# ALiBi attention: the bias enters the scores' bank on TensorE, and the scores get two banks

## What is computed

```
    def _L1_attn_ref(x, Wq, Wk, Wv, Wo):
...
        q = (x @ Wq).reshape(B, T, N_HEAD, HEAD_DIM).transpose(0, 2, 1, 3)
        k = (x @ Wk).reshape(B, T, N_HEAD_KV, HEAD_DIM).transpose(0, 2, 1, 3)
        v = (x @ Wv).reshape(B, T, N_HEAD_KV, HEAD_DIM).transpose(0, 2, 1, 3)
        k = jnp.repeat(k, rep, axis=1)
        v = jnp.repeat(v, rep, axis=1)
        scale = 1.0 / math.sqrt(HEAD_DIM)
        att = jnp.einsum('bhqd,bhkd->bhqk', q, k) * scale
...
        alibi = slopes[:, None, None] * rel[None, :, :].astype(jnp.float32)
        alibi = jnp.repeat(alibi, rep, axis=0)[:N_HEAD]
        att = att + alibi[None]
        causal = jnp.triu(jnp.full((T, T), -jnp.inf, dtype=jnp.float32), k=1)
        att = att + causal[None, None]
        att = jax.nn.softmax(att.astype(jnp.float32), axis=-1).astype(q.dtype)
        y = jnp.einsum('bhqk,bhkd->bhqd', att, v)
        y = y.transpose(0, 2, 1, 3).reshape(B, T, C)
        return y @ Wo
...
    x = x + _L1_attn_ref(_layernorm(x, axis=-1), L1_attn_Wq, L1_attn_Wk, L1_attn_Wv, L1_attn_Wo)
```

## Time and profile before

| | |
|---|---|
| median of 3 runs | 1994.62 us (1993.47 to 1998.78) |
| profiled execution, its own time | 1999.79 us |
| its span in the profile | 1997.6 us |
| TensorE busy in the span | 1700.9 us (85%) |
| VectorE busy | 1510.0 us (76%) |
| ScalarE busy | 1031.7 us (52%) |
| GpSimd busy | 712.7 us (36%) |
| the stage's first normalise starts, its last addition ends | 1019.85 us, 1171.66 us |

### The profile page before, as it was taken

One profiled execution on the slowest core, in us unless ns is written; L12 is line 12 of the kernel. 1 busy time (PEld: TensorE's weight loads), 2 busy tenths in 40 slices (PEclk: granted clock), 3 DMA queues, 4 the chain that ended last, 5 costly groups with the idle time before them and its releaser, 6 DMA issues. The chain is left out here.

```text
span 1997.6 us, 43307 instructions
## 1 busy us (share of the span) xinstructions
PE 1700.9 (85%) x15744; PEld 1000.6 (50%) x15744; DVE 1510.0 (76%) x2875; ACT 1031.7 (52%) x2056; POOL 712.7 (36%) x935
## 2 busy tenths in 40 slices
PE   5999999599999999899747737777777599999998
PEld 2666665267777777745434412222222246656565
DVE  5766666689989899668859969888899268675754
ACT  3666666255555555344336726777778333323222
POOL 4644321586777667313433343434431000000000
PEclk9999999799999999999979978999999799999999
DMA  9601100100000000000001112322321012222221
GB/s 240 166 28 49 28 7 2 62 14 9 15 10 12 6 9 1 1 1 1 1 29 41 37 27 74 83 80 83 95 67 39 23 41 94 88 69 70 67 77 53
DMA packets 87661, 94.91 MB, mean 48 GB/s; under 512 B 17568, under 2 KB 63264, under 8 KB 87456
## 3 DMA queue, kind: packets, MB, share of 16 engines
q1 hardware_dynamic: 83712, 87.76, 15.8%
q10 hardware_dynamic: 2976, 2.32, 0.5%
q0 software_dynamic: 768, 2.10, 0.3%
HBM read 78.51 MB, written 10.22 MB: 44 GB/s over the span
## 5 line engine op out<-in xcount | busy, mean ns | idle before, releaser
L205 PE MATMUL ps<-arena 128*128 128x512 f16 (+6 forms) x6464 | 1091.1, 324 | 57.2 <-DVE arena L1800 14.0
L205 PEld LDWEIGHTS ps<-arena 128*128 128x128 f16 (+1 forms) x6464 | 603.7, 99 | 444.7 <-issue 41.7
L1477 DVE TENSOR_REDUCE arena<-ps 128x4 f32<-128x1024 f32 x256 | 305.0, 1218 | 46.4 <-PE ps L1390 46.4
L1460 ACT ACTIVATE arena<-ps 128x512 f32<-128x512 f32 x512 | 278.4, 597 | 107.4 <-PE ps L1398 87.3
L1390 PE MATMUL ps<-arena 31*128 31x256 f16 x1024 | 107.1, 288 | 106.5 <-ACT arena L1460 47.0
L1445 PE MATMUL ps<-arena 128*32 128x256 f32 x2048 | 170.8, 407 | 2.4 <-ACT arena L1467 0.6
L2221 DVE TENSOR_TENSOR arena<-ps,arena 128x512 f32<-128x512 f32 x96 | 66.2, 690 | 118.7 <-ACT arena L2094 90.6
L2094 ACT ACTIVATE arena<-ps 128x512 f32<-128x512 f32 x96 | 57.2, 596 | 184.7 <-PE ps L205 184.4
L1390 PEld LDWEIGHTS ps<-arena 31*128 31x128 f16 x1024 | 34.8, 93 | 228.4 <-DVE arena L1477 132.7
L968 POOL TENSOR_TENSOR arena<-arena 128x512 f32<-128x512 f32 x96 | 98.7, 1041 | 44.8 <-DVE arena L156 43.7
L1398 PE MATMUL ps<-arena 32*128 32x256 f16 x1024 | 104.8, 284 | 1.5 <-ACT arena L1460 0.4
(11 more groups left out here) (199 smaller groups left out, 2911.8 us busy)
## 6 DMA issues: line engine op xcount, KB each, us to landing
arena<-moe_cw SPq DMA_DIRECT2D x64, 192.0 KB, 2.9
arena<-moe_cw SPq DMA_DIRECT2D x64, 128.0 KB, 3.0
arena<-in_L_ffn_gate_up_proj SPq DMA_DIRECT2D x16, 384.0 KB, 3.6
ch_out<-arena SPq DMA_DIRECT2D x32, 128.0 KB
arena<-moe_cw SPq DMA_DIRECT2D x64, 64.0 KB, 2.8
ch_keys<-arena SPq DMA_DIRECT2D x48, 64.0 KB, 2.0
arena<-ch_keys SPq DMA_DIRECT2D x64, 48.0 KB
arena<-arena SPq DMA_DIRECT2D x192, 16.0 KB
```

What stands on the lines that cost most here:

```text
L205: last = nc.tensor.matmul(out, a, b, start=start and n == 0, stop=stop and n == len(pairs) - 1, skip_group_check=not group)
L1460: nc.scalar.activation(pT[:, b % 3, g], ps[:, T[n % len(T)], :].rearrange("p (u t) -> p u t", u=KD), ACT.Exp, scale=CH_SCALE).then_inc(s_e ...
L1477: nc.vector.tensor_reduce(m[:, half % 2, 2 * half_pair:2 * half_pair + 2, j, :], ps[:, bank(user):bank(user) + 2, :].rearrange("p g (u s) ...
```

## The change

L1790 is taken out of VectorE's program, and TensorE adds the bias instead. Before the loop, VectorE splits the bias into three bf16 pieces (each the rounding of what the pieces before leave over) and makes a bf16 identity. For each unit TensorE then first multiplies the identity by each of the three pieces into the scores' bank, and adds the scores onto that. The factor 0.25 moves into ScalarE's copy of the queries. The maximum and the shift read the bank directly; the shift writes `logits`, and the exponential is taken in place (`e = logits`), so the shift waits for GpSimd's product two units before. The scores use two banks in turn; TensorE waits for the shift of two units before. For that a bank is freed: keys and values are projected into one, and the wait for `v_kept` comes ahead of the keys' products.

```
-    LNB, QB, KB_, VB, SC, PT, O, ACC = range(8)
+    LNB, QB, KVB, PT, O, ACC = 0, 1, 2, 5, 6, 7
+    SC = (3, 4)
...
+    parts = sb("parts", [P, ALIBI_PARTS, ALIBI_KVH * S], BF16)
+    ident = sb("ident", [P, P], BF16)
+    logits, prob = (sb(c, [P, 2, 8, S], F32) for c in ("logits", "prob"))
+    e = logits
...
+                        pe.wait_ge(v_kept.sem, v_kept.at(i, s))
                         pe.wait_ge(k_kept.sem, k_kept.at(i, s))
...
-                        pe.wait_ge(v_kept.sem, v_kept.at(i, s))
...
-                        pe.wait_ge(biased.sem, biased.at(i, k))
+                        pe.wait_ge(s_bias, 2 * ALIBI_PARTS)
+                        pe.wait_ge(shifted.sem, shifted.at(i, k - 1))
+                        for n in range(ALIBI_PARTS):
+                            nc.tensor.matmul(ps[:, SC[k % 2], :].rearrange("p (r n) -> p r n", r=2), ident[:, :], parts[:, n, :].unsqueeze(1).broadcast_to([P, 2, ALIBI_KVH * S]),
+                                             start=n == 0, stop=False, skip_group_check=True)
                         for b in range(2):
-                            last = nc.tensor.matmul(ps[b * S:(b + 1) * S, SC, :], qT[:, s % 2, a, b * S:(b + 1) * S],
-                                                    kT[:, s % 2, b].rearrange("p h k -> p (h k)"), start=True, stop=True)
+                            last = nc.tensor.matmul(ps[b * S:(b + 1) * S, SC[k % 2], :], qT[:, s % 2, a, b * S:(b + 1) * S],
+                                                    kT[:, s % 2, b].rearrange("p h k -> p (h k)"), start=False, stop=True, skip_group_check=True)
...
-                        nc.scalar.activation(qT[:, s % 2], ps[:, QB, 0:D].rearrange("p (a q) -> p a q", a=ALIBI_PAIRS), ACT.Copy).then_inc(q_kept.sem, 1)
+                        nc.scalar.activation(qT[:, s % 2], ps[:, QB, 0:D].rearrange("p (a q) -> p a q", a=ALIBI_PAIRS), ACT.Copy, scale=ALIBI_SCALE).then_inc(q_kept.sem, 1)
...
+            nc.vector.tensor_copy(ident, core.ident).then_inc(s_bias, 1)
+            left = bias.rearrange("p g k -> p (g k)")
+            for n in range(ALIBI_PARTS):
+                nc.vector.tensor_copy(parts[:, n, :], left).then_inc(s_bias, 1)
+                dve.wait_ge(s_bias, 2 * n + 2)
+                if n < ALIBI_PARTS - 1:
+                    nc.vector.tensor_tensor(left, left, parts[:, n, :], ALU.subtract).then_inc(s_bias, 1)
+                    dve.wait_ge(s_bias, 2 * n + 3)
...
-                        dve.wait_ge(exped.sem, exped.at(i, k - 1))
-                        nc.vector.scalar_tensor_tensor(out=lg.rearrange("p (r g) k -> p r (g k)", r=2), in0=ps[:, SC, :].rearrange("p (r n) -> p r n", r=2),
-                                                       scalar=ALIBI_SCALE, in1=bias.rearrange("p g k -> p (g k)").unsqueeze(1).broadcast_to([P, 2, ALIBI_KVH * S]),
-                                                       op0=ALU.mult, op1=ALU.add).then_inc(biased.sem, 1)
-                        dve.wait_ge(biased.sem, biased.at(i, k + 1))
-                        nc.vector.tensor_reduce(top[:, k % 2, :], lg, AX.X, ALU.max).then_inc(maxed.sem, 1)
+                        nc.vector.tensor_reduce(top[:, k % 2, :], sc, AX.X, ALU.max).then_inc(maxed.sem, 1)
                         dve.wait_ge(maxed.sem, maxed.at(i, k + 1))
-                        nc.vector.tensor_tensor(lg, lg, spread(top[:, k % 2, :], S), ALU.subtract).then_inc(shifted.sem, 1)
+                        dve.wait_ge(probs.sem, probs.at(i, k - 1))
+                        nc.vector.tensor_tensor(logits[:, k % 2], sc, spread(top[:, k % 2, :], S), ALU.subtract).then_inc(shifted.sem, 1)
```

More of the change, by code:

```diff
@@ L1574 @@
 ALIBI_SCALE = 0.25
+ALIBI_PARTS = 3
 ALIBI_KV = ALIBI_KVH * ALIBI_HD
@@ L1604, in alibi_stage @@
     scored = tally("scored", ALIBI_UNITS)
-    biased, maxed, shifted, totalled, inverse = (tally(c, ALIBI_UNITS) for c in ("biased", "maxed", "shifted", "totalled", "inverse"))
+    maxed, shifted, totalled, inverse = (tally(c, ALIBI_UNITS) for c in ("maxed", "shifted", "totalled", "inverse"))
     exped, probs = tally("exped", ALIBI_UNITS), tally("probs", ALIBI_UNITS)
@@ L1609, in alibi_stage @@
     projected, added = tally("projected", SUBS), tally("added", SUBS)
-    s_const, s_zero = core.sem("al_const"), core.sem("al_zero")
+    s_const, s_zero, s_bias = core.sem("al_const"), core.sem("al_zero"), core.sem("al_bias")
     c_in = [core.sem("al_c_in0"), core.sem("al_c_in1")]
@@ L1622, in alibi_stage @@
     bias = sb("bias", [P, ALIBI_KVH, S], F32)
-    logits, e, prob = (sb(c, [P, 2, 8, S], F32) for c in ("logits", "e", "prob"))
+    parts = sb("parts", [P, ALIBI_PARTS, ALIBI_KVH * S], BF16)
+    ident = sb("ident", [P, P], BF16)
+    logits, prob = (sb(c, [P, 2, 8, S], F32) for c in ("logits", "prob"))
+    e = logits
     top, total, inv = (sb(c, [P, 2, 8], F32) for c in ("top", "total", "inv"))
@@ L1683, in body @@
                         last.then_inc(q_ready.sem, 1)
+                        pe.wait_ge(v_kept.sem, v_kept.at(i, s))
                         pe.wait_ge(k_kept.sem, k_kept.at(i, s))
                         for c in range(KD):
-                            last = product(nc, ps[:, KB_, 0:P], [q[:, c, :] for q in w.k], [q[:, c, :] for q in x], c == 0, c == KD - 1)
+                            last = product(nc, ps[:, KVB, 0:P], [q[:, c, :] for q in w.k], [q[:, c, :] for q in x], c == 0, c == KD - 1)
                         last.then_inc(k_ready.sem, 1)
-                        pe.wait_ge(v_kept.sem, v_kept.at(i, s))
                         for c in range(KD):
-                            last = product(nc, ps[:, VB, 0:ALIBI_KV], [q[:, c, :] for q in x], [q[:, c, :] for q in w.v], c == 0, c == KD - 1)
+                            last = product(nc, ps[:, KVB, P:P + ALIBI_KV], [q[:, c, :] for q in x], [q[:, c, :] for q in w.v], c == 0, c == KD - 1)
                         last.then_inc(v_ready.sem, 1)
@@ L1748, in body @@
                                 last = nc.scalar.activation(v[c * S:(c + 1) * S, s % SUBS, b, :, c * ALIBI_HD:(c + 1) * ALIBI_HD],
-                                                            ps[b * S:(b + 1) * S, VB, 0:ALIBI_KV].rearrange("p (g c d) -> p g c d", c=2, d=ALIBI_HD)[:, :, c, :], ACT.Copy)
+                                                            ps[b * S:(b + 1) * S, KVB, P:P + ALIBI_KV].rearrange("p (g c d) -> p g c d", c=2, d=ALIBI_HD)[:, :, c, :], ACT.Copy)
                         last.then_inc(v_kept.sem, 1)
@@ L1752, in body @@
                         for j in range(8):
-                            last = nc.scalar.activation(kT[:, s % 2, :, j, :], ps[:, KB_, 0:P].rearrange("p (b k) -> p b k", b=2), ACT.Copy,
+                            last = nc.scalar.activation(kT[:, s % 2, :, j, :], ps[:, KVB, 0:P].rearrange("p (b k) -> p b k", b=2), ACT.Copy,
                                                         scale=core.headmask[:, j:j + 1])
@@ L1772, in _ @@
             settle(core, dve, "al")
-            credit(dve, normed, x_lo, biased, maxed, shifted, totalled, inverse, o_lo, added)
+            credit(dve, normed, x_lo, maxed, shifted, totalled, inverse, o_lo, added)
             nc.vector.memset(v, 0.0).then_inc(s_zero, 1)
             dve.wait_ge(s_zero, 1)
+            dve.sem_inc(s_zero, 1)
             dve.wait_ge(s_const, 16)
-            dve.sem_inc(s_zero, 1)
+            nc.vector.tensor_copy(ident, core.ident).then_inc(s_bias, 1)
[6 more added lines that the diff above has]
+                    dve.wait_ge(s_bias, 2 * n + 3)
             def body(i, alive):
@@ L1786, in body @@
                     if alive(k):
[L1787 removed]
+                        sc = ps[:, SC[k % 2], :].rearrange("p (h k) -> p h k", k=S)
                         dve.wait_ge(scored.sem, scored.at(i, k + 1))
[L1789 to L1794 removed]
+                        nc.vector.tensor_reduce(top[:, k % 2, :], sc, AX.X, ALU.max).then_inc(maxed.sem, 1)
                         dve.wait_ge(maxed.sem, maxed.at(i, k + 1))
[L1796 removed]
+                        dve.wait_ge(probs.sem, probs.at(i, k - 1))
+                        nc.vector.tensor_tensor(logits[:, k % 2], sc, spread(top[:, k % 2, :], S), ALU.subtract).then_inc(shifted.sem, 1)
                     k, s, a = unit(t, L_TURN)
```

1 line of the change is left out of this document (removed).

## The result

| | before | after |
|---|---|---|
| median | 1994.62 us | 1986.22 us |
| runs, lowest to highest | 15, 1991.23 to 2000.1 | 15, 1981.47 to 1992.1 |
| profiled execution, its own time | 1999.79 us | 1987.77 us |
| stage, first clearing to last statistics (profiles) | 152.48 us | 142.36 us |
| its 13 intervals of pair 0 | 111.11 us | 100.09 us |

The ratio is 0.9954, with a 95% interval of 0.9943 to 0.9966: 8.4 us by the medians, 7 to 11 by the interval, against 9.3 forecast. The stage is counted from the clearing of the values (L1774, now L1783) to the end of the last statistics (L162) on VectorE; 1171.66, given as the end of the last addition in the table of the kernel before, is the end of these statistics, and the addition ends at 1171.08.

A forecast was written before the change was run, and what follows sets the result against it. A loop through VectorE and TensorE, 8.14 us per sub-tile, was taken as the bound. Seven terms sum to -9.3 us: 1990.5 for an execution like the profiled one, 1985.3 against the median 1994.62; 8-in-10 range 1980 to 1992.5.

The forecast's parts named there:

- The loop of 8.14 us and the walk to 7.69: One sub-tile's loop through VectorE and TensorE: 8.14 us before, 7.69 after by hand-walk, gaining 0.45 per regular interval.
- Making the pieces, +2.1: Before the first normalise, VectorE builds the three bias parts and identity once, in the open: +2.1 us, bounds 1.5 and 3.
- The first block at a lowered clock, +1.0: TensorE's first bias block, at the stage's start, runs at a lowered clock: 0.65 x 1.5, +1.0 us.
- First interval -0.2, regular intervals -5.9, turns of the loop -1.5: First interval, still filling, -0.2 us; 13 regular intervals at 0.45 each, -5.9; step loop's turns, -1.5 of 1.9.
- allowance of +1.1 for ties: Mix, L1812 and projections each come within 0.15 us of a second condition: 0.08 x 14, +1.1 us.
- Tail -2.5: Tail without projections, VectorE alone leading: unit 28 hands on 0.4 us sooner, three behind it 0.72 each; -2.5 us.
- Falls of the clock, -3.4: Three falls of TensorE's clock in the 13 intervals, about 1.1 us each, vanish as its holes are nearly filled: -3.4 us.
- terms 1 to 5: Pieces +2.1, first block +1.0, first interval -0.2 and regular ones -5.9, loop turns -1.5, tail -2.5 us.
- Rival A: TensorE's clock falls stay in the stage, each costing some 0.4 us more: total change -4.7, 1989.9 us; chance 0.20.
- Rival B: Shift's new wait for GpSimd's product, or another tie, keeps intervals at 8.14: 1991.2 us, to 1994 without term 6; chance 0.10.
- Rival C: TensorE's bias products do not stream, each costing its full 0.389 us: slower, 2001 us; chance 0.08.
- D: Bias products hidden better in TensorE's waits, 1973 us, or about 1978.5 at 0.131 us each; chance 0.07.

The follow-up runs named there:

- early products: Changed kernel with three pieces, the next unit's bias products issued right after a unit's scores; interval 7.43 us, ratio 0.9920 to the kernel before.
- both savings: Changed kernel with two f16 pieces in place of three bf16, issued right after the scores of the unit before; interval 7.11 us, ratio 0.9913.
- two f16 pieces: Changed kernel with two f16 bias pieces in place of three bf16 ones, mask constant -3e4; interval 7.40 us, ratio 0.9921 to the kernel before.
- the kernel with the filled hole: Kernel before plus ten unread f16 products of 128x256 after pair 1's scores, in TensorE's 1.38 us hole; stage 149.03 us, ratio 0.9990.

## Why the prediction was right, and where it was not

The time was right, 1985.3 against 1986.22, and so was its likeliest mechanism. By its own steps:

1. *The loop of 8.14 us and the walk to 7.69.* Right: 7.68. The experiments with three and six products (7.68, 8.98) and with one bank (8.21) confirm what bounds it. That two thirds of VectorE's saving of 1.44 go to the two bias blocks is not borne out: without them the interval is 7.11 and not 8.14 - 1.44 = 6.70, so the blocks take 0.57, and 0.41 could not be had as ScalarE's path binds. For the experiments the regular interval was forecast by the same walk, and with early products by TensorE's load, taken from the kernel without products. It was right to 0.01 with six products and with both savings, within 0.11 with early products and with one bank, and wrong by 0.15 and 0.3 with two f16 pieces and with no products, where a third engine came on the loop that the walk had left out: GpSimd's product and ScalarE's key copies.
2. *Making the pieces, +2.1.* 2.0.
3. *The first block at a lowered clock, +1.0.* 1.3. The factor of 1.5 came from the first scores, in the course of which the clock rises (1.61 us before, 1.66 after, 1.08 at the full clock); the block stands ahead of them, wholly at the lower level, and took 1.9 times its time.
4. *First interval -0.2, regular intervals -5.9, turns of the loop -1.5.* The first went from 6.98 to 6.89. 107.6 without falls to 100.1 is -7.5; a turn costs 7.76 - 7.68 = 0.08 instead of 0.64. The 1.9 us of the turns were not three of 0.64: the profiles without falls show two of 0.64, one interval with 0.32 more and small rests; the total is the same. The allowance of +1.1 for ties was not needed: the mix and its low half wait for nothing in a regular interval, and the projections only for L1813, as in the walk.
5. *Tail -2.5.* 21.3 to 19.0 is -2.3.
6. *Falls of the clock, -3.4.* This is the step that was wrong as put. The falls are not a cost that the kernel pays each time: in the four profiles with its holes they cost some 3.4 us in two and nothing in the other two. Counted in full, the term belongs to the one profiled execution; the prediction took it off the median of the runs as well. Against that, the prediction left out that the clock also falls in the tail of the kernel before, at 2.7 us, in three of the four. The rule behind it (the Trainium skill, TensorE: Matmul & The Clock Gate, Part 1: recent activity releases the throttle) agrees with where the falls come, behind idle time; that the same idle time brings a fall in one execution and none in another is what the profiles add.

Without any fall the stage goes from 149.0 (the kernel with the filled hole; the kernel before comes to the same by its parts without a fall, 13.06, 6.98, 107.63 and 21.32) to 142.4, which is 6.6 us; this part is shown, by two equal profiles of each and by the steps: terms 1 to 5 were forecast at -7.0. That the whole came out at 8.4 against 9.3 is in part luck: the allowance and the term of the clock gave -2.3 together, and something worth 1.8 stood in their place in the medians.

The medians show more, and that holds for all seven kernels with the products or without them: set against the 149.03 of the stage without falls, their stages differ by -6.7 (after), -12.9, +13.3, +3.4, -9.3, -11.3 and -14.5 us (none, six, one bank, two f16, early, both), while their ratios times 1994.62 give -9.2, -16.6, +10.4, +2.6, -15.8, -16.0 and -17.4. Each is lower than its stage explains, by 0.8 to 6.4 us, 3.4 in the mean; in two of them, the 3.7 without products and the 6.4 with two f16 pieces, 1.5 us or more of that is the fall in the first interval, which their one profile has. The stages of the kernel before, in its three profiles, lie 4.0 above 149.03 in the mean, which is the same size.

The rest of the program is a rival for these microseconds. The profiled spans less their stages give it 1843.1 us in the mean of the three profiles of the kernel before and 1843.2 in the eight of the changed kernel and its variants, so no difference shows; but single ones lie between 1837.1 and 1845.5, as far apart as what is to be explained. So the clock is probably worth some 2 to 4 us over many executions; that is argued from few profiles, not shown, and how often it falls stays open. The ratio of the filled kernel, 2 us below 1 and with an interval that touches it, speaks neither clearly for it nor against it.

Rival A (the falls stay) did not happen in two profiles. Rival B (the wait for GpSimd) was absent by its margin of 0.17 us, and present with two f16 pieces; with the products issued early it is absent again, though the loop is as short or shorter (7.43 and 7.11 against 7.40). Rival C is ruled out by the 0.215 us from one product to the next, D by that and by the interval of 7.68. That TensorE would be above 90 and VectorE near 82 of 100 us came out as 96.5 and 83.1.

## What to carry to other kernels

An engine that is busy 90% of a stage can still be only one part of a loop through two engines: lay out one period from the timelines, and price what is added to the other engine on the same loop before counting what is taken away. Work that nobody waits for yet is worth moving to where its engine waits: issuing the same products one unit earlier gained 0.25 us per sub-tile, having a third fewer 0.28. A cost of the clock that is read off one profile needs a second profile of the same kernel before it is counted, and before an experiment that makes it vanish is believed.

## What the runs showed of the hardware

- Products of 128x512 with an f32 sum in PSUM stream at 0.216 us each at the full clock, in bf16 with a repeated operand and followed by f32 products as well, and six of them cost twice what three do.
- VectorE's maximum and subtraction over 512 values take 0.69 us from a bank of PSUM as from memory.
- The 24 projections of one sub-tile take 1.35 us at the full granted clock and 2.38 us where it is at its lower level.
- At the same place, after the same idle time (1.94 and 1.95 us of it in TensorE's hole at a turn of the loop), the granted clock fell to its lower level in one execution of the same kernel and stayed up in another; the intervals without a fall agreed to 0.02 us.
